# Five adjacency loads issued as 120 and 8 partitions, and an earlier catch-up batch, in a sparse graph-attention kernel

## The reference

```python
h = jnp.maximum(_layernorm(x, axis=-1), 0.0)
h = h @ W
s_src, s_dst = h @ a[:128, 0], h @ a[128:, 0]
e = leaky_relu(s_src[:, None] + s_dst[None, :], 0.2)
e = jnp.where(adj > 0, e, -9e15)
out = x + jax.nn.softmax(e, axis=1) @ h
```

## Time and profile before

| What | Value |
|---|---|
| Median of 3 runs | 799.86 us (799.39 to 799.94) |
| Profiled execution, its own time | 800.1 us |
| Profiled execution, span | 798.3 us |
| DVE busy | 598.9 us, 75% of the span |
| ACT, POOL, PE busy | 66%, 64%, 63% |
| DMA: bytes moved, mean rate | 299.33 MB, 375 GB/s |
| Load of two units: from issue to landing, median | 18.7 us |

### The profile page before, as it was taken

How to read it: one execution, slowest core, us unless ns; L and a number is a source line. 1 busy time by engine, 2 the same in 40 slices (tenths; PEclk the granted TensorE clock), 3 DMA queues, 4 the chain that set the end, 5 groups by cost and what they waited for, 6 DMA issues and landing times.

```text
span 798.3 us, 8948 instructions
## 1 busy us (share of the span) xinstructions
PE 505.1 (63%) x1823; PEld 230.5 (29%) x1855; DVE 598.9 (75%) x3132; ACT 526.8 (66%) x372; POOL 509.7 (64%) x520
## 2 busy tenths in 40 slices
PE   3677566666666566857766667667756766666621
PEld 3562222222222123323222223222322322322321
DVE  7957568766776767787767887677786787999893
ACT  3869767676767676676766677767677676767400
POOL 4653777656666665577766655655667776577672
PEclk9989758667667776585566766765577677586655
DMA  8999999999999999999999999999999999999510
GB/s 330 425 392 396 405 404 409 407 409 411 405 408 410 405 409 412 403 395 401 397 394 392 390 407 398 393 394 399 387 403 400 395 392 389 391 405 362 210 49 16
DMA packets 41127, 299.33 MB, mean 375 GB/s; under 512 B 11014, under 2 KB 13985, under 8 KB 24688
## 3 DMA queue, kind: packets, MB, share of 16 engines
q1 hardware_dynamic: 23264, 276.83, 85.9%
q0 software_dynamic: 15264, 17.60, 6.9%
q10 hardware_dynamic: 2544, 4.33, 1.5%
HBM read 304.18 MB, written 8.65 MB: 392 GB/s over the span
## 4 chain that ended last, share of the span: by engine, by line
DMA 53%; DVE 15%; issue 12%; ACT 9%; POOL 6%; PE 4%; POOLq 0%; ACTq 0%; DVEq 0%
DMA adj_buf<-in_adj 51%; ACT mask_buf L487 8%; POOL gathered L380 5%; DVE x_all L876 4%; PE banks L1108 2%; DVE stats L592 2%; DMA gathered<-table,index 1%; PE banks L1071 1%; POOL w_gathered L405 1%; DVE mv_all L596 1%; DVE rest L670 1%; DVE work L926 1%; DVE words L672 1%; DMA x_all<-in_x 1%; DVE words L668 0%
## 5 line engine op out<-in xcount | busy, mean ns | idle before, releaser
L487 ACT ACTIVATE mask_buf<-adj_buf,minus_half 128x2048 bf16<-128x2048 int32 x251 | 488.5, 1994 | 203.2 <-DMA adj_buf<-in_adj 202.7
L380 POOL DMA_INDIRECT gathered<-table,index x446 | 446.2, 1000 | 240.4 <-issue 144.8
L1108 PE MATMUL banks<-mask_buf,bit_ident 128*128 128x512 bf16 x992 | 378.3, 526 | 113.6 <-ACT mask_buf L487 110.3
L1108 PEld LDWEIGHTS banks<-mask_buf,bit_ident 128*128 128x128 bf16 x1024 | 107.7, 124 | 329.9 <-ACT mask_buf L487 192.6
L876 DVE SCALAR_TENSOR_TENSOR x_all<-gathered,weight,x_all 128x128 f32<-128x128 f32 x508 | 156.3, 348 | 7.0
L668 DVE MAX8 words<-banks 128x8 f32<-128x512 f32 x64 | 44.7, 698 | 124.0 <-PE banks L1108 123.9
L1104 PE MATMUL banks<-key_rows,ones_b 3*128 3x512 bf16 x64 | 32.2, 503 | 118.7 <-ACT mask_buf L487 118.2
L1149 PE MATMUL banks<-x_all,one_hot 128*128 128x128 f32 x128 | 43.7, 443 | 9.0 <-DVE x_all L876 9.0
L1104 PEld LDWEIGHTS banks<-key_rows,ones_b 3*128 3x128 bf16 x64 | 6.1, 95 | 140.3 <-ACT mask_buf L487 138.8
L672 DVE MAX8 words<-rest 128x8 f32<-128x512 f32 x64 | 44.5, 695 | 2.2
L670 DVE MATCH_REPLACE8 rest<-words,banks 128x512 f32<-128x512 f32 x64 | 43.5, 680 | 0.0
(11 more groups left out here) (169 smaller groups left out, 537.6 us busy)
## 6 DMA issues: line engine op xcount, KB each, us to landing
adj_buf<-in_adj SPq DMA_DIRECT2D x127, 2048.0 KB, 18.7
gathered<-table,index POOLq DMA_INDIRECT x446, 6.4
table<-gathered ACTq DMA_DIRECT2D x4, 1040.0 KB, 14.6
x_all<-in_x SPq DMA_DIRECT2D x3, 1024.0 KB, 10.9
out<-x_all SPq DMA_DIRECT2D x2, 1280.0 KB, 6.8
x_all<-in_x SPq DMA_DIRECT2D x2, 512.0 KB, 5.1
adj_buf<-in_adj SPq DMA_DIRECT2D x1, 1024.0 KB, 17.8
adj_buf<-in_adj SPq DMA_DIRECT2D x2, 512.0 KB, 17.1
```

Source lines behind the costliest of these rows:

```text
L380: nc.gpsimd.indirect_dma_start(g_cols[buf][:, k, :], None, table, bass.IndirectOffsetOnAxis(index[:, buf, k:k + 1], 0), bounds_check=N, oo ...
L487: nc.scalar.activation(mask_buf[:, u], adj_buf[:, u], ACT.Sign, bias=minus_half[:]).then_inc(mask_ready, 1)
L1108: ins = mm(bank, bit_ident[:, h * PART_BITS + c], mask_buf[:, u, c * BIT_COLS:(c + 1) * BIT_COLS], start=False, stop=(h == PARTS - 1 and c ...
```

## The change

Five of the 128 full loads, those of units 2 and 3 in batches 4, 10, 16, 22 and 28, are issued as two DMAs: partitions 0 to 119, and partitions 120 to 127, which count on a semaphore of their own (`rest_loaded`). ACT waits for that one too before it masks these units. And `CATCH_UP` is 25 in place of 28.

```diff
+IN_TWO = ((4, 2), (10, 2), (16, 2), (22, 2), (28, 2))
+MOST = P - 8
...
-CATCH_UP = 28
+CATCH_UP = 25
...
             def load_two(i, u):
                 source = rows_of(adj, i * BATCH + u // PARTS, 1)[:, 0, u % PARTS * PART:(u % PARTS + 2) * PART]
-                sp.dma_start(adj_buf[:, u:u + 2, :].rearrange("p u n -> p (u n)"), source).then_inc(adj_loaded[u // 2], 16)
+                place = adj_buf[:, u:u + 2, :].rearrange("p u n -> p (u n)")
+                if (i, u) in IN_TWO:
+                    sp.dma_start(place[0:MOST], source[0:MOST]).then_inc(adj_loaded[u // 2], 16)
+                    sp.dma_start(place[MOST:P], source[MOST:P]).then_inc(rest_loaded, 16)
+                else:
+                    sp.dma_start(place, source).then_inc(adj_loaded[u // 2], 16)
...
             def mask(i, u):
                 act.wait_ge(adj_loaded[u // 2], 16 * (i + 1))
+                if (i, u // 2 * 2) in IN_TWO:
+                    act.wait_ge(rest_loaded, 16 * (IN_TWO.index((i, u // 2 * 2)) + 1))
```

More of the change, by code:

```diff
@@ L224, in gat_kernel @@
         end_loaded, end_masked = [sem(f"end_loaded{h}") for h in range(2)], sem("end_masked")
+        rest_loaded = sem("rest_loaded")
         adj_loaded = [sem(f"adj_loaded{k}") for k in range(UNITS // 2)]
```

## The result

| | us |
|---|---|
| before, median of 4 runs beside the changed kernel | 799.81 (799.39 to 799.94) |
| changed kernel, median of 4 runs | 867.55 (863.34 to 868.77) |
| ratio | 1.0835, 95% interval 1.081 to 1.086 |
| forecast | 784 (779 to 796) |

The change costs 67.7 us. The forecast had the sign wrong, and even the rival on the slower side was far too cheap.

The account below looks back on a forecast made before the run. The prediction took adjacency loads, paced by one lagging DMA engine, as the bound. From 800.1 us it took 19.8 for the faster pace, added 3.5 for ninth shares and 0.5 for the catch-up: 784.3, forecast 784 us, range 779 to 796.

Parts of the forecast that it names:

- the rival on the slower side: Rival 3: the laggard gets a ninth share at the five splits, 3.5 us slower, 803.4 us; chance 12%.
- One engine lags and sets the pace of 22.64 us: Adjacency loads: one of 16 DMA engines finishes some 6 us behind the others, so batches take 22.64 us.
- I take the first: 120 partitions dealt eight to an engine leave one engine out; if it lags, it is spared 28.3 us of work.
- rival 3: Five split loads: the laggard gets the ninth share of the small piece, 3.5 us slower, 803.4 us; chance 12%.
- What the pieces bring depends on how they are dealt to engines: Five split loads: pieces charged by shares of 0.71 us; eight engines get a ninth share, 3.5 us lost.
- The bounds of 28.3 us either way: Large piece: the laggard spared 28.3 us of work, or given 28.3 us more if 120 partitions go to eight engines.
- SP's five issues and ACT's added wait cost nothing: Five added issues of 0.33 us on SP and ACT's extra wait: no cost while each engine has more than one load queued.
- Without the laggard the pace is 21.92 us: Loads from batch 4 on: 21.92 us a batch in place of 22.64, saving 19.8 us over 27.5 batches.
- The catch-up: CATCH_UP in batch 25: gather waits of 8 us, DVE 2 to 5 us late at batch 28, 0.5 us on the sum.
- Rival 2: Nothing changes: the laggard isn't spared and gets no share more, or pieces fall on the same engines; 800 us; chance 8%.

Follow-up runs that it names:

- extra4: Kernel before, plus a small DMA of 4 rows of 3 KB behind each of 111 full loads from batch 4 on: 815.44 us, ratio 1.0187.
- extra3: Kernel before, plus a small DMA of 3 rows of 3 KB behind each of 111 full loads from batch 4 on: 798.67 us, ratio 0.9986.
- split_only: Changed kernel with CATCH_UP back at 28, so only the five loads split into 120 and 8 partitions: 867.43 us, ratio 1.0838.
- columns_two: Kernel before, the five loads in two DMAs by columns, each of all 128 partitions, second on rest_loaded: 801.6 us, ratio 1.0013.
- near120: Split kernel with CATCH_UP 28, the 120-partition piece reading rows 16 KB apart in place of 128 KB: 866.87 us, ratio 1.0802.
- far128: Kernel before, the five loads in one piece but reading rows 256 KB apart in place of 128 KB: 799.3 us, ratio 0.998.
- halves: Split kernel with CATCH_UP 28, the five loads cut into 64 and 64 partitions: 858.23 us, ratio 1.0726.
- piece112: Split kernel with CATCH_UP 28, the five loads cut into 112 and 16 partitions: 854.73 us, ratio 1.0682.
- low64: Kernel before, the five loads fetching only partitions 0 to 63 in one DMA: 823.63 us, ratio 1.0286.
- mid64: Kernel before, the five loads fetching only partitions 32 to 95 in one DMA: 790.26 us, ratio 0.9869.
- spare3: Kernel before, six loads with their last 512 columns in three DMAs of 123, 3 and 2 partitions: 817.56 us, ratio 1.0209.
- spare4: Kernel before, four loads with their last 1024 columns in 32 DMAs of 4 partitions on four engines: 817.44 us, ratio 1.0226.
- extra1: Kernel before, plus a small DMA of one 3 KB row behind each of 111 full loads from batch 4 on: 800.61 us, ratio 1.001.

## Why the prediction was wrong, point by point

1. **One engine lags and sets the pace of 22.64 us: borne out.** extra4 costs 16 us where extra3 costs nothing, and the single-engine tail is still there in the profile after.
2. **"I take the first", that the engine left out of the 120 partitions is the laggard: wrong.** The laggard is the fourth engine, and the one left out is the last, if the lowest-numbered carry the pieces. So it kept its eight shares of the large piece and got a ninth of the small one. The condition of rival 3 holds. Its price of 5 x 0.71 = 3.5 us can be but a small part of the loss of 67.3.
3. **"What the pieces bring depends on how they are dealt to engines": here the sum failed.** The deal itself fits, 15 and 8 (35 packets). But the sum charged the two pieces by shares alone, at 0.71 us a share whatever partitions are written: 5 x 0.71 = 3.5 us for all five. No row showed that, and there was no term for the rate at which the engines write when their partitions are not those of a load of 128. Measured are 67.3 us, 13.5 a split (split_only), and 169 GB/s in place of 407 at the same DMA share. The bounds of 28.3 us either way, taken from shares too, could not hold it. It is not the number of DMAs (columns_two) nor the distance of the rows read (near120, far128), and it needs no piece on fewer engines (halves, piece112). That the partitions written at one time set the rate is shown for 64 of them (low64 against mid64), and for the split it is the reading that is left. The map of ports had no part in the sum.
4. **SP's five issues and ACT's added wait cost nothing: right** (columns_two has both).
5. **Without the laggard the pace is 21.92 us: the size is that of the other engines' pace**, seen behind pauses in spare3 (21.9) and spare4 (22.0). That sparing the laggard gives it is not shown, and this change never reached it: 22.5 us between splits. Of the 19.8 us nothing came.
6. **The catch-up: right in kind, too dear in size.** Gather waits came (4.3 us for 8), POOL's wait is shorter, and 1.55 us of cover are left. Its 0.5 us can't be told from nothing (0.9979 to 1.0004). In the changed kernel late loads give DVE so much room that it plays no part.
7. **Rival 2, nothing changes: wrong.** It leaned on the Trainium skill, "DMA: Bandwidth & Descriptors", "Rules for kernel authors", that two transfers to disjoint halves serialize and are not worth it. halves agrees that they are not, and shows that they cost 11.6 us a load, where the rival had 800 us in all.

How the 13.5 us come about is argued, not shown. Suppose that engines work in step, that those on one port take turns, and that each takes a run of neighbouring partitions when a piece hasn't 128. By the map of the Trainium skill, "SBUF — State Buffer", "Door 1: The DMA port swizzle", 120 partitions then have 15 engines on 8 ports, at most two on each, so 16 times a share of 0.71 us; the eight of the small piece have two ports, four on each, another 4. Against 8 for a whole load that is 12 x 0.71 = 8.5 us more; for halves 8 x 0.71 = 5.7, for 112/16 10 x 0.71 = 7.1, and for low64 over mid64 4 x 0.71 = 2.8 us. Measured are 13.5, 11.6, 10.9 and 6.7. These estimates leave 4 to 6 us of each unexplained, which may be that the load ahead is written out of step with the pieces (the 7.17 us at 125.10). No run separates this part, nor was the supposed deal of partitions seen. Open are also why the fourth engine lags (the instruction fetches fit in size, 23.5 to 23 us, and were not tested), and why 112/16 costs less than halves although the map has it dearer.

## What to carry to other kernels

If a load must be cut in a kernel that is bound by DMA, cut it along the free dimension, not across partitions: two DMAs of all 128 partitions cost nothing here; two of 64, or of 120 and 8, cost 11 to 13.5 us a load. Before an engine is spared, find out which one lags: here a small DMA of N rows behind each load, with N varied from run to run, told it. And read the DMA share beside GB/s, since engines at a share of 1.0 moved anything from 142 to 407 GB/s.

## What the runs showed of the hardware that was not expected

- While 64 partitions are written in one DMA, the engines move 170 to 175 GB/s at 0 to 63 and 398 to 403 GB/s at 32 to 95.
- One engine, the fourth, has no slack while the first three have 15 us of it (extra3 798.67, extra4 815.44).
- Rows read 256 KB apart in the five loads cost nothing (far128, 0.998).
- A DMA of a single 3 KB row has (26816 - 23264) / 111 = 32 packets (extra1), which fits a row cut over all 16 engines.
